# A two-block kernel (causal attention, then a routed mixture of experts): the last block is opened without GpSimd's drain at its end

## The chip, the cores and the metric

The kernel runs on one core of one Trainium2 chip. The metric is device time in microseconds of one execution, and the number before is the median of three runs. Five engines take part, each with an instruction queue of its own: TensorE (PE), VectorE (DVE), ScalarE (ACT), GpSimd (POOL) and SyncE (SP). Transfers run beside them on 16 DMA engines.

## What is computed

The reference, cut to what matters. The input is 4 sequences of 1024 tokens with 256 features; the result has the same shape.

```python
x = layernorm(x + attention(x))      # 16 heads of 16, causal, softmax
x = layernorm(x + ffn(x))

def ffn(x):                          # E = 16 experts, K = 2 per token, F = 128
    scores = sigmoid(x @ gate_w)
    _, selected = top_k(scores + expert_bias, K)
    w = scores[selected] / (scores[selected].sum() + 1e-20)
    shared = silu(x @ shared_gate_w) * (x @ shared_up_w) @ shared_down_w
    for e in range(E):
        g, u = split(x @ experts_gate_up[e])
        routed += comb[:, e] * (silu(g) * u @ experts_down[e])
    return shared + routed
```

## The kernel before

The program is written per engine, with semaphores by hand, in two blocks. A block (`nc.Block()`) holds one body for each engine. Its entry and its exit belong to a `with` context, and the exit of a block emits a barrier over all five engines. In the profile the instructions of that exit are booked to the line of the `with` statement in which the block was entered: L425 (`with ExitStack() as c1`) for the first block and L895 (`with ExitStack() as c3`) for the last one.

The barrier works through two semaphores, gather and release. Four engines (ScalarE, TensorE, DVE, SyncE) each run a DRAIN, which adds 1 to gather, and then a semaphore instruction that waits for release. GpSimd runs a DRAIN of its own, then a semaphore instruction that waits until gather is 4, then one that adds 4 to release. There are three such barriers: one at the start of the program (L1565), one at the end of the first block (L425) and one at the end of the last block (L895). Behind the last one the program has nothing more.

The first block projects q, k and v, and runs the attention in 16 steps (a batch and a group of four heads each). GpSimd masks probabilities there and copies values; it starts no transfer.

The last block does the output projection, the first layernorm, routing, the shared expert, the routed experts and the second layernorm, in this order:

- GpSimd sorts rows by expert with 64 indirect transfers (`scatter`, L1083: 40 for the first section of the tokens, 24 for the second) into `y_sorted`, and after each pair of expert blocks it sends the two results home with indirect transfers (`send_home`, L1091: 96 in all) into `z_back`.
- SyncE loads the sorted rows and later the two results of each tile (`load_z`, L1021).
- DVE adds the weighted results for each of the 32 tiles (`combine`, L1347 and L1350) and takes their statistics (L1353, L1355).
- GpSimd turns the statistics of four tiles into scale and shift (`second_deviation`, L1099 to L1104), in nine parts; the last two parts hold two tiles each.
- ScalarE applies them (`second_norm`, L1188) and sends the finished chunk to `out` (L1196) for seven of the eight chunks. SyncE sends the two halves of the last chunk (L1051).
- SyncE's last instructions of the block wait until all output transfers have landed (L1054):

```python
for c in range(CHUNKS):
    sp.wait_ge(out_stored[c], 16 * sum(part[0] == c for part in PARTS))
```

GpSimd's last instructions of the block are those of `second_deviation` for the last part. Everything that its indirect transfers write has been waited for earlier, since the results are read back from `z_back`.

Of the kernel before, what the change touches and what calls it, by code (L numbers as in the profile page):

```python
# [207 lines left out]
def build(nc, x, xT, Wq, bq, Wk, bk, Wv, bv, Wo, bo, gate_w, expert_bias, sg_w, su_w, sd_w, gu_w, down_w, out):  # L208
    with ExitStack() as ctx:
# [215 lines left out]
        with ExitStack() as c1:  # L425
# [226 lines left out]
            blk = c1.enter_context(nc.Block())  # L652
# [242 lines left out]
        with ExitStack() as c3:  # L895
# [110 lines left out]
            COUNT_BANK = 7  # L1006
            PARTS = [(c, 0, CT) for c in range(CHUNKS - 1)] + [(CHUNKS - 1, 0, CT // 2), (CHUNKS - 1, CT // 2, CT)]

            blk = c3.enter_context(nc.Block())

            @blk.sync
            def _(sp):
# [562 lines left out]
```

How the kernel before makes its waits and increments, by code:

```python
def wait_count(eng, sem, value):  # L163
    if isinstance(value, int) and value <= 0:
        return
    eng.wait_ge(sem, value)
# [2 lines left out]
def wait_apart(eng, sem, value, waited):  # L170
    eng.wait_ge(sem, value)
    eng.sem_inc(waited, 1)
# [165 lines left out]
        def turn_maxima(pe, i, qc, bank):  # L340
            pe.wait_ge(m_ready[qc], i + 1)
            dst = ps[0:3 * GH, bank, :].bitcast(BF16)
            for t in range(CT):
                mm = pe.transpose(dst[:, t * P:(t + 1) * P],
                                  m_parts[:, qc * CT + t].rearrange("p r h -> p (r h)"), ident_b[:, :])
            mm.then_inc(mT_ready[qc], 1)
# [1 line left out]
        def piece_maximum(dve, i, n, bank):  # L348
            qt, h, heads, half, w = MAXES[n]
            dst = m_neg[:, qt, h:h + heads] if half == 0 else m_neg_late[:, qt - CT, h:h + heads]
            if masked_by_vector(n):
                scores = ps[:, bank, 0:w]
                wait_apart(dve, score_max_ready, NM * i + n + 1, dve_waited)
                dve.tensor_tensor_reduce(out=scores, in0=scores, in1=wide_mask[:, CH - w:], scale=-1.0, scalar=-NEG,
                                         op0=ALU.add, op1=ALU.min, accum_out=dst).then_inc(reduced, 1)
                return
            dve.wait_ge(score_max_ready, NM * i + n + 1)
            dve.tensor_reduce(dst, ps[:, bank, 0:heads * w].rearrange("p (h k) -> p h k", h=heads), AX.X, ALU.max,
                              negate=True).then_inc(reduced, 1)
```

## Time and profile before

| | us |
|---|---|
| median of 3 runs | 894.93 |
| lowest and highest of them | 894.47, 896.44 |
| the profiled execution's own time | 893.04 |
| its span, first to last instruction | 891.3 |
| TensorE busy | 818.8 |
| DVE busy | 643.1 |
| ScalarE busy | 484.3 |
| GpSimd busy | 341.4 |

The page and its views count an engine as busy only with operations that it executes on data. Drains, branches and semaphore instructions run on an engine's sequencer (marked with a q, as POOLq); they appear where a single line is asked for, and in the chain and the waits, but not in the timeline or the busy times. The execution's own time is 1.7 us longer than its span; what lies outside the span isn't in the trace.

### The profile page before, as it was taken

The numbers are of one execution on the slowest core, as the hardware profiler recorded it, in microseconds if no ns is written. First come the engines' busy times: TensorE is split into PE (matmuls) and PEld (weight loads), VectorE is DVE, ScalarE is ACT, GpSimd is POOL, SyncE is SP. The second block draws the span as 40 slices with busy tenths as digits, with TensorE's granted clock in tenths as the row PEclk, the third lists the DMA queues.
The fourth block names the chain that finished last, engine by engine and source line by source line (L and its number), as shares of the span: only waits on it lengthen the run. The fifth ranks groups of instructions, "written<-read, shape, count | busy, mean of one in ns | idle before, by whom it ended". The sixth has DMA issues, their size and how long they took to land. (4 is left out here: it accounts for less than half of the span.)

```text
span 891.3 us, 17342 instructions
## 1 busy us (share of the span) xinstructions
PE 818.8 (92%) x5250; PEld 456.0 (51%) x5251; DVE 643.1 (72%) x1747; ACT 484.3 (54%) x728; POOL 341.4 (38%) x464
## 2 busy tenths in 40 slices
PE   7987999999999999999999999899996999999910
PEld 3554534434434343434443443389663888888810
DVE  6346899999999999999999996168775222227774
ACT  2443367667666766666666765656521344444443
POOL 5442412111221122111211122276477777655583
PEclk9999999999999999999999999999898899999965
DMA  8698363587556644685235500136133666567855
GB/s 275 211 251 190 124 91 41 105 144 105 90 109 108 97 63 107 120 145 71 37 39 72 74 1 4 50 124 204 43 108 106 211 185 187 174 183 233 273 181 207
DMA packets 90442, 114.60 MB, mean 129 GB/s; under 512 B 9232, under 2 KB 70928, under 8 KB 90384
## 3 DMA queue, kind: packets, MB, share of 16 engines
q1 hardware_dynamic: 74176, 85.22, 45.0%
q0 software_dynamic: 7680, 21.11, 6.5%
q10 hardware_dynamic: 8528, 7.50, 2.6%
q8 instruction: 36, 0.59, 0.3%
q14 instruction: 22, 0.18, 0.1%
HBM read 62.74 MB, written 50.66 MB: 127 GB/s over the span
## 5 line engine op out<-in xcount | busy, mean ns | idle before, releaser
L734 ACT ACTIVATE work<-ps 128x1024 f32<-128x1024 f32 (+3 forms) x384 | 293.8, 809 | 154.3 <-PE ps L805 151.9
L689 POOL TENSOR_SCALAR_AFFINE_SELECT work<-work 128x512 f32<-128x512 f32 x128 | 81.2, 634 | 371.7 <-ACT work L734 371.7
L358 DVE TENSOR_REDUCE m_neg<-ps 128x1 f32<-128x512 f32 (+2 forms) x304 | 195.1, 684 | 8.3 <-PE ps L334 5.3
L354 DVE CUSTOM_DVE_ANT_0 ps<-ps,wgu 128x384 f32<-128x384 f32 (+1 forms) x256 | 154.3, 649 | 15.2 <-PE ps L334 14.8
L334 PE MATMUL ps<-stacks 96*128 96x512 bf16 (+3 forms) x528 | 144.7, 329 | 8.0 <-DVE m_neg L354 4.6
L805 PE MATMUL ps<-stacks 99*128 99x512 bf16 (+3 forms) x528 | 125.4, 326 | 2.2 <-ACT work L734 1.7
L820 PE MATMUL ps<-work,vg 128*32 128x512 f32 (+3 forms) x1056 | 110.8, 497 | 0.4 <-POOL work L689 0.2
L1091 POOL DMA_INDIRECT z_back<-v_home,home x96 | 92.3, 962 | 47.5 <-ACT v_home L1165 27.4
L334 PEld LDWEIGHTS ps<-stacks 96*128 96x128 bf16 x528 | 49.2, 97 | 100.6 <-DVE m_neg L358 33.0
L1485 PE MATMUL ps<-wgu,work 128*128 x384 | 92.0, 383 | 0.0
L1333 DVE TENSOR_TENSOR work<-work,ps 128x256 f32<-128x256 f32 x48 | 20.2, 422 | 93.1 <-ACT work L1159 93.1
L1485 PEld LDWEIGHTS ps<-wgu,work 128*128 128x128 f32 x384 | 70.1, 192 | 8.0 <-issue 0.2
L805 PEld LDWEIGHTS ps<-stacks 99*128 99x128 bf16 x528 | 44.0, 98 | 53.9 <-ACT work L734 14.7
L1083 POOL DMA_INDIRECT y_sorted<-v_home,row_of x64 | 61.9, 966 | 23.1 <-issue 18.0
L615 PE MATMUL ps<-work,wqk 128*128 128x512 f32 x128 | 60.6, 613 | 7.5 <-DMA wqk<-in_Wq 5.6
L334 PE MATMUL ps<-wgu 96*128 96x512 bf16 (+3 forms) x240 | 65.9, 328 | 0.0
L505 POOL TENSOR_TENSOR work<-work 128x512 bf16<-128x512 f32 x32 | 36.4, 1156 | 66.5 <-ACT work L538 66.5
L805 PE MATMUL ps<-wgu 99*128 99x512 bf16 (+3 forms) x240 | 57.3, 326 | 0.0
L533 ACT ACTIVATE work<-ps,bqk 128x512 bf16<-128x512 f32 x32 | 21.8, 685 | 53.7 <-DMA qk_parts<-work 36.3
L820 PE MATMUL ps<-work 128*32 128x512 f32 (+3 forms) x480 | 50.4, 497 | 0.0
L1501 PE MATMUL ps<-wdn,work 128*128 x192 | 49.6, 381 | 0.8 <-DVE work L1339 0.8
L574 DVE SCALAR_TENSOR_TENSOR work<-ps,bqk,work 128x512 f32<-128x512 f32 x32 | 23.9, 749 | 35.8 <-ACT work L533 35.7
(142 smaller groups left out, 1156.0 us busy)
## 6 DMA issues: line engine op xcount, KB each, us to landing
stacks<-qk_parts SPq DMA_DIRECT2D x132, 128.0 KB, 6.8
work<-y_sorted SPq DMA_DIRECT2D x48, 260.0 KB
qk_parts<-work SPq DMA_DIRECT2D x32, 384.0 KB, 5.1
y_sorted<-wgu SPq DMA_DIRECT2D x7, 1560.0 KB, 7.9
work<-z_back SPq DMA_DIRECT2D x32, 256.0 KB, 3.8
wgu<-qk_parts SPq DMA_DIRECT2D x60, 128.0 KB, 6.2
work<-in_xT SPq DMA_DIRECT2D x8, 512.0 KB, 4.3
work<-in_x SPq DMA_DIRECT2D x8, 512.0 KB, 4.0
```

The costliest lines, as they stand in the source:

```text
L334: mm = pe.matmul(dst, qs[r][0:KS, h0 + m, qt * P:(qt + 1) * P], ks[r][0:KS, h0 + m, half * CH:half * CH + w], start=True, stop=not diag)
L354: dve.tensor_tensor_reduce(out=scores, in0=scores, in1=wide_mask[:, CH - w:], scale=-1.0, scalar=-NEG, op0=ALU.add, op1=ALU.min, accum_out ...
L358: dve.tensor_reduce(dst, ps[:, bank, 0:heads * w].rearrange("p (h k) -> p h k", h=heads), AX.X, ALU.max, negate=True).then_inc(reduced, 1)
L615: mm = pe.matmul(ps[:, t, :], wqk[:, t // 2, h, (t % 2) * P:(t % 2 + 1) * P], xt[c % 3][:, h, :], start=(h == 0), stop=(h == DC - 1))
L689: pool.affine_select(out=blk_, in_=blk_, compare_op=ALU.is_ge, fill=0.0, base=0, pattern=[[0, GH], [1, P]], channel_multiplier=-1).then_in ...
L734: act.activation(probs[:, s + 2 * pair:s + 2 * pair + 2, off:CH], ps[:, SCORE_BANK + 2 * pair:SCORE_BANK + 2 * pair + 2, off:CH], ACT.Exp, ...
L805: mm = pe.matmul(ps[:, SCORE_BANK + h, off:CH], ks[r][0:KM, h, kt * P:(kt + 1) * P], qs[r][0:KM, h, qc * CH + off:(qc + 1) * CH], start=Tr ...
L820: mm = pe.matmul(ps[32 * h:32 * h + 32, OUT_BANK, off:CH], vg[r][:, kt, h, :], probs[:, s + h, off:CH], start=(kt == 0), stop=(kt == CT * ...
L1083: pool.indirect_dma_start(out=y_sorted[g], out_offset=bass.IndirectOffsetOnAxis(ap=row_of[:, j, t:t + 1], axis=0), in_=y_rows_all[:, t, :] ...
L1091: pool.indirect_dma_start(out=z_back, out_offset=bass.IndirectOffsetOnAxis(ap=home[:, 2 * n + k:2 * n + k + 1], axis=0), in_=zs[n % ZS][:, ...
L1485: mm = pe.matmul(ps[:, 2 + r, 2 * F * k:2 * F * (k + 1)], ysT[r][:, h, k, :], wgu[:, bass.ds(e, 1), h, :].squeeze(1), start=(h == 0), stop ...
L1501: mm = pe.matmul(ps[:, 6 + r, D * k:D * (k + 1)], hxT[r][:, k, :], wdn[:, bass.ds(e, 1), :].squeeze(1), start=True, stop=True)
```

## The change

The last block is opened with `no_gpsimd_drain=True`.

```diff
             COUNT_BANK = 7
             PARTS = [(c, 0, CT) for c in range(CHUNKS - 1)] + [(CHUNKS - 1, 0, CT // 2), (CHUNKS - 1, CT // 2, CT)]
 
-            blk = c3.enter_context(nc.Block())
+            blk = c3.enter_context(nc.Block(no_gpsimd_drain=True))
 
             @blk.sync
             def _(sp):
```

In the built program this changes only the barrier at the end of that block; all other instructions and their order are the same. This is what each engine has there:

```
engine                  before                                after
ACT, PE, DVE, SP        DRAIN, which adds 1 to gather         DRAIN
                                                              EVENT_SEMAPHORE, which adds 1 to gather
                        EVENT_SEMAPHORE, waits for release    EVENT_SEMAPHORE, waits for release
POOL                    DRAIN                                 (none)
                        EVENT_SEMAPHORE, waits gather >= 4    EVENT_SEMAPHORE, waits gather >= 4
                        EVENT_SEMAPHORE, adds 4 to release    EVENT_SEMAPHORE, adds 4 to release
```

The first block and the barrier at the start of the program stay as they are.

## Rows read from the trace of the kernel before

**Rows 1.** The page: its head and the busy times by engine.

```profile
span 891.3 us, 17342 instructions
PE 818.8 (92%) x5250; PEld 456.0 (51%) x5251; DVE 643.1 (72%) x1747; ACT 484.3 (54%) x728; POOL 341.4 (38%) x464
```

**Rows 2.** Timeline from 880.5 us: start, duration, engine, line, operation.

```profile
880.51 3.16 SPq L1051 DMA_DIRECT2D out<-stacks  x2
...
881.95 0.19 POOL L1104 TENSOR_TENSOR second_moments<-second_moments,second_rstd 128x2 f32<-128x2 f32 x1
882.17 1.09 ACT L1188 ACTIVATE stacks<-stacks,second_moments,second_rstd 128x256 f32<-128x256 f32 x2 [1.69 <-POOL second_moments L1104]
```

**Rows 3.** Busy time of each engine by stretch, with clock, DMA share, GB/s.

```profile
880.00:884.00 4.00, 0.00 (x0) 0.00 (x0) 0.41 (x2) 1.58 (x3) 1.36 (x4) 0.50 0.53 178
884.00:886.00 2.00, 0.00 (x0) 0.00 (x0) 0.00 (x0) 0.00 (x0) 0.00 (x0) 0.50 0.40 135
886.00:888.00 2.00, 0.00 (x0) 0.00 (x0) 0.00 (x0) 0.00 (x0) 0.00 (x0) 0.50 0.00 0
888.00:892.00 4.00, 0.00 (x0) 0.00 (x0) 0.00 (x0) 0.00 (x0) 0.00 (x0) 0.50 0.00 0
```

**Rows 4.** Line L895: count, ns min/median/max, first and last start in us.

```profile
L895 POOLq EVENT_SEMAPHORE  x2: 17/17/17, 891.1 to 891.2; - x2
L895 PEldq DRAIN  x1: 1027/1027/1027, 850.6 to 850.6; - x1
L895 DVEq DRAIN  x1: 220/220/220, 880.3 to 880.3; - x1
L895 POOLq DRAIN  x1: 9152/9152/9152, 881.9 to 881.9; - x1
L895 ACTq DRAIN  x1: 1121/1121/1121, 882.2 to 882.2; - x1
L895 SPq COMPARE_BRANCH  x1: 41/41/41, 885.8 to 885.8; - x1
L895 SPq DRAIN  x1: 7/7/7, 885.9 to 885.9; - x1
L895 SPq EVENT_SEMAPHORE  x1: 17/17/17, 891.2 to 891.2; - x1
```

**Rows 5.** The chain that ended last, its last pieces: start, us, what.

```profile
881.91 0.24 POOLq L895
...
882.77 0.49 ACTq L895
```

**Rows 6.** Waits of SyncE: us in total, times, longest.

```profile
SPq L895 <- PEq L895: 5.3, 1, 5.3
...
SPq L1054 <- DMA out<-stacks: 1.5, 1, 1.5
```

**Rows 7.** Line L425, the end of the first block, columns as in rows 4.

```profile
L425 POOLq EVENT_SEMAPHORE  x2: 17/17/17, 575.8 to 575.8; - x2
...
L425 POOLq DRAIN  x1: 3264/3264/3264, 572.4 to 572.4; - x1
...
L425 DVEq DRAIN  x1: 464/464/464, 575.2 to 575.2; - x1
```

**Rows 8.** Timeline of GpSimd from 574 to 577 us.

```profile
573.54 2.09 POOL L407 TENSOR_TENSOR work<-work,bo_all 128x256 f32<-128x256 f32 x3
575.97 0.34 POOL L1071 IOTA v_home<- 128x128 int32 x1 [0.34 <-POOLq L425]
```

**Rows 9.** Groups of GpSimd by line: its indirect transfers; busy, mean ns, idle before.

```profile
L1091 POOL DMA_INDIRECT z_back<-v_home,home x96 | 92.3, 962 | 47.5 <-ACT v_home L1165 27.4 <-issue 19.2 <-DVE home L1328 0.9
...
L1083 POOL DMA_INDIRECT y_sorted<-v_home,row_of x64 | 61.9, 966 | 23.1 <-issue 18.0 <-DVE row_of L1299 4.0 <-POOL v_home L1071 1.1
```

**Rows 10.** Timeline of GpSimd from 854 to 858 us.

```profile
856.27 0.96 POOL L1091 DMA_INDIRECT z_back<-v_home,home  x1 [0.30 <-issue]
857.31 0.35 POOL L1099 TENSOR_SCALAR second_rstd<-second_moments 128x4 f32<-128x4 f32 x1
```

**Rows 11.** Line L1565, the barrier at the start: GpSimd's drain.

```profile
L1565 POOLq DRAIN  x1: 173/173/173, 0.4 to 0.4; - x1
```

## The prediction, made before the changed kernel had run

> **What bounds the end now.** The change touches only the last microseconds, so I read the views from the end backwards and use the middle of the kernel only as a yardstick. First the page's head: the span, first to last instruction, is 891.3 us, with TensorE busy 92% of it [rows 1]. None of that work is touched; TensorE's last matrix work lies well ahead of the stretch in question.
>
> Next the timeline from 880.5 us on [rows 2]. GpSimd's last recorded operation (L1104) starts at 881.95 and takes 0.19, so it ends at 882.14. ScalarE's last (L1188) ends at 882.17 + 1.09 = 883.26. SyncE issues the last output transfer right behind it. The table by stretches says the same of the end [rows 3]: no engine has recorded work after 884, the transfers stop before 886, and from 886 on there is neither work nor traffic. Yet the span runs to 891.3. More than 5 us are idle on every row that counts as busy.
>
> What fills them shows only where the sequencers' own instructions are listed, at L895, the `with` line to which the exit of the last block is booked [rows 4]. DVE's drain starts at 880.3 and takes 0.22; ScalarE's starts at 882.2 and takes 1.12 (until its ACTIVATEs are done); SyncE's starts at 885.9 and takes 0.007. GpSimd's starts at 881.9 and takes 9.152, so it ends at about 881.91 + 9.15 = 891.06; the chain of waits puts GpSimd's sequencer at L895 from 881.91, which gives the second decimal [rows 5]. All semaphore instructions of the barrier stand behind it, at 891.1 and 891.2. TensorE's started at 850.6 and was over after 1.03.
>
> SyncE's waits confirm who is late [rows 6]. It waited 1.5 us at L1054 for the output to land, and then 5.3 us at L895 for the barrier. The releaser named there is TensorE's sequencer, whose drain had been over since 851.6, so the name is a guess of the view; the only drain still running after 885.9 is GpSimd's. The chain of waits also stops at ScalarE's last ACTIVATE and books nothing to the drain, so the page's list by line hides this cost.
>
> **Is that long drain only waiting for GpSimd's operations?** The first block ends in the same sort of barrier, at L425, and gives the comparison [rows 7]. There GpSimd's drain starts at 572.4 and takes 3.264, ending at 575.66; its last operation (the group of L407 at 573.54 for 2.09 us) ends at 575.63 [rows 8]. The drain ended 0.03 us after the work. In the last block it ends 891.06 - 882.14 = 8.92 us after it. What lies between the two is GpSimd's indirect transfers: 64 of L1083 and 96 of L1091 [rows 9], all in the last block. The last of the 96 was issued at 856.27 and was done on GpSimd in 0.96 us; arithmetic followed at once, at 857.31 [rows 10]. So whatever the 8.92 us are, they did not keep GpSimd from small operations during the 25 us before.
>
> **The change part by part.**
>
> 1. GpSimd's drain leaves the end of the last block. The barrier then closes when the latest of the other arrivals comes in. Those are TensorE (851.6), DVE (880.5), GpSimd itself (after its last operation is handed out, about 881.9), ScalarE (883.3) and SyncE, whose branch to the block's end stands at 885.8 and whose drain starts at 885.9 [rows 4]. SyncE is now last, because it alone waits for the output. That cover ends there: no other engine hides anything behind it.
>
> 2. From the last arrival to the end of the span. Before: 891.29 (the timeline's span is 891.3) - 891.06 = 0.23 us from the drain's end. In the first block, DVE's drain was last: 575.2 + 0.46 = 575.7, and the first operations start at 575.97 [rows 7, 8], 0.3 us later. I take 0.27, between the two.
>
> 3. Four other engines get one more instruction each: the drain now carries no semaphore, and a semaphore instruction follows. Only SyncE's lies on the path. Such instructions take 0.017 us there [rows 4], and two neighbouring ones of SyncE (the branch and the drain) start 0.1 apart; so 0.02 to 0.1, and I take 0.07. Nothing else is queued behind it on SyncE.
>
> 4. Nothing moves in the program ahead of the block's end, so no queue, buffer or clock changes. The other two barriers keep their drains: at the start 0.17 us and at L425 hidden behind DVE's last work [rows 7, 11].
>
> The sum: the span ends at 885.9 + 0.01 + 0.07 + 0.27 = 886.25 instead of 891.3, which is 5.05 us less. From SyncE's side: of its wait of 5.3, 0.27 + 0.07 stay, leaving 4.96. I take **5.0 us**. The profiled execution took 893.04 with a span of 891.3, so 1.7 us lie around it; the new profiled time is 888.0. That execution was 1.9 us under the median of the three runs, 894.93. The same 5.0 off the median gives **889.9 us**, or -0.56%. The bounds of the sum alone are 4.9 (the larger values of items 2 and 3) and 5.1.
>
> **What the drain does in 8.92 us, and a rule beside it.** The two drains show 0.03 us behind ordinary operations, and 8.92 us behind a block with 160 indirect transfers. Nothing before shows which of two things that is: work that runs whether or not somebody asks, or work that the drain itself starts. The sum above assumes that after the change nobody inside the measured time asks. If someone does, the price lies between nothing saved and the whole 8.92 moved behind the barrier.
>
> The Trainium skill (PSUM — Partial Sum Buffer, Engine vs sequencer instructions) says that a drain waits for the engine to go fully idle. By that rule read with the recorded operations alone, the drain would end at about 882.2, ahead of SyncE, and the change would save nothing. The trace disagrees by 8.9 us: either GpSimd isn't idle when its recorded operations end, or the drain does more.
>
> **The rivals.**
>
> A. Nothing gained: the 8.92 us are work under way in GpSimd from 882.14 on, drain or not, and something behind the barrier but inside the measured time waits until GpSimd is idle. The end stays at 891.06 plus what followed it: profiled 893.0, median 894.9. For it: this kernel's time holds 1.7 us outside the span, so something is done there. Against it: that something was short, and GpSimd took arithmetic at once behind its indirect transfers [rows 10], which doesn't look like an engine with a backlog. The same time results if GpSimd's semaphore instruction were held in the drain's place.
>
> B. Slower: the 8.92 us start only when somebody asks for GpSimd's idleness, and the next to ask sits behind the barrier, inside the measured time. Before, the asking began at 882.14 and 3.8 us of the work lay beside the output transfer and SyncE's wait (885.9 - 882.14). Moved behind the barrier, it starts at 886.25 and ends at 895.17, 4.1 us later than 891.06: profiled 897.2, median **899.0**, +0.46%. It decides if the asking is inside the measured time at all; its start would have to be before 882.14 for the move to cost nothing. For it: the difference of 0.03 and 8.92 fits something that a drain does for indirect transfers. Against it: it needs a second wait for idleness, and the 1.7 us around the span leave little room for one.
>
> The Trainium skill names a place for such a wait. Runtime: NRT & Kernel Launch (The ~15µs preamble/postamble breakdown) lists a barrier behind the kernel in which all engines are waited for, about 1.5 us, and VectorE: DVE Perf Modes (The DRAIN you can't avoid) counts drains of some 12 ns on all five engines outside the kernel. By the first page, A or B would hold; by the 12 ns of the second, nothing is left to pay. No row here shows what lies outside the span.
>
> C. That the change does nothing at all would need GpSimd's drain still at the block's end. The built program has none there, so only A covers this case.
>
> **How the numbers follow.** A measurement of this kernel tells about 0.2% from no change, here 1.8 us. The forecast (the wait for GpSimd is gone and isn't paid again inside the measured time) gets 0.80, because the room outside the span is small and the idle gap is seen whole in the trace. A gets 0.11. B gets 0.07, as it needs both a drain that starts the work and a second asker. The last 0.02 is a part of the wait coming back, still faster. So faster 0.82, same 0.11, slower 0.07.
>
> The three runs of before spread over 2.0 us, from 894.47 to 896.44, and the profiled one lay 1.9 us under their median. A median of few runs after may well sit 1 us off on either side, which makes 888.4 to 891.4 around 889.9. To leave out no more than 2 in 10, I stretch it toward A: 888.3 to 892.6.
>
> **What the changed profile would show.** At L895 no drain of GpSimd; SyncE's drain near 885.9 with the semaphore instructions 0.1 to 0.3 us behind it; SyncE's wait at L895 down from 5.3 to about 0.3; a span of about 886.2; stretches up to 884 as before. If the span is 886.2 but the time outside it grew from 1.7 to 6.8, A holds; if it grew to about 11, B does. If the span is not shorter, GpSimd's semaphore instruction waits in the drain's place. A shift elsewhere, before 880 us, would make the prediction wrong in a way that it has no term for.

## The result and the profile after

The changed kernel takes 889.32 us (median of six runs, 887.19 to 891.82), before 894.87 (six runs, 894.02 to 896.79). The ratio is 0.9931, with a 95% interval of 0.9912 to 0.9950: 4.5 to 7.9 us less. (The ratios here and below are those on record with their intervals, and not quotients of the medians; that quotient is 0.9938 here.) The forecast of 889.9 us lies 0.6 us off, and its 5.0 us lie inside the interval.

Line L895 of the changed kernel, to be held against [rows 4] (count, ns min/median/max, first and last start in us):

```profile
L895 PEldq EVENT_SEMAPHORE  x2: 51/51/51, 852.5 to 887.0; - x2
L895 DVEq EVENT_SEMAPHORE  x2: 21/21/21, 881.4 to 887.0; - x2
L895 ACTq EVENT_SEMAPHORE  x2: 17/17/17, 884.2 to 887.0; - x2
L895 SPq EVENT_SEMAPHORE  x2: 17/17/17, 886.8 to 887.0; - x2
L895 POOLq EVENT_SEMAPHORE  x2: 17/17/17, 886.8 to 886.9; - x2
...
L895 DVEq DRAIN  x1: 220/220/220, 881.1 to 881.1; - x1
L895 ACTq DRAIN  x1: 1119/1119/1119, 883.0 to 883.0; - x1
L895 SPq COMPARE_BRANCH  x1: 41/41/41, 886.6 to 886.6; - x1
L895 SPq DRAIN  x1: 7/7/7, 886.7 to 886.7; - x1
```

There is no drain of GpSimd. Each of the other four has its drain and now two semaphore instructions, the first of which is the arrival: 852.5, 881.4, 884.2, and for SyncE 886.8. GpSimd's own stand at 886.8 and 886.9, and everybody is released at 887.0. SyncE is the last to arrive, as forecast. Its waits in the changed kernel, against [rows 6]:

```profile
SPq L1054 <- DMA out<-stacks: 1.4, 1, 1.4
...
SPq L895 <- PEq L895: 0.2, 1, 0.2
```

The wait at the exit went from 5.3 to 0.2 us; the wait for the output's landing is as long as it was (1.5 and 1.4). This 5.1 us is the gain, read inside each of the two executions.

The two spans, 891.3 and 887.0, differ by 4.3 only:

```profile
span 887.0 us, 17345 instructions
PE 817.8 (92%) x5250; PEld 455.8 (51%) x5251; DVE 643.0 (72%) x1747; ACT 484.2 (55%) x728; POOL 341.7 (39%) x464
```

The work ahead of the end was 0.8 us later in this execution than in that of before: DVE's drain starts at 881.1, not 880.3. Whole executions of one kernel differ by more than that, so I measure the end from a mark inside the same execution, the start of DVE's drain at L895 to the end of the span. It is 11.0 us before (891.3 - 880.3) and 5.9 after (887.0 - 881.1). The execution's own time was 888.77, 1.8 us over its span, against 1.7 before, which is the same within the rounding of the spans. Nothing was pushed out of the span.

### The profile page after: what moved, and what is told of

Read it like the earlier page. It is cut to its first block and busy times, and to the rows that moved or that the text cites. A ratio compares the mean times of both kernels' runs of the same rounds, so it can differ in the third digit from the quotient of the medians.

```text
span 887.0 us, 17345 instructions
## 1 busy us (share of the span) xinstructions
PE 817.8 (92%) x5250; PEld 455.8 (51%) x5251; DVE 643.0 (72%) x1747; ACT 484.2 (55%) x728; POOL 341.7 (39%) x464
## 5 line engine op out<-in xcount | busy, mean ns | idle before, releaser
L354 DVE CUSTOM_DVE_ANT_0 ps<-ps,wgu 128x384 f32<-128x384 f32 (+1 forms) x256 | 154.3, 649 | 15.3 <-PE ps L334 14.8
```

The lines of the kernel that those rows point to most:

```text
L354: dve.tensor_tensor_reduce(out=scores, in0=scores, in1=wide_mask[:, CH - w:], scale=-1.0, scalar=-NEG, op0=ALU.add, op1=ALU.min, accum_out ...
```

## The experiments

### The changed kernel once more

No edit. It was timed again beside further runs of the kernel before.

> The changed kernel once more, for a tighter ratio. Theory 1 (SyncE's wait for GpSimd's drain is gone, 5.0 us, nothing comes back): ratio 0.9944, about 889.9 against 894.9, and 1.7 to 1.8 us outside the span. Rival (something else gained too, since the medians first measured differ by 5.55): a ratio clearly under 0.993.

Measured: 891.07 against 894.98, ratio 0.9937 (0.9914 to 0.9961), own time 1.7 us over its span. The profiled execution of this very kernel had a span of 891.3 us, as long as that of before:

```profile
L895 DVEq DRAIN  x1: 220/220/220, 885.3 to 885.3; - x1
```

By the mark the end is 891.3 - 885.3 = 6.0 us, as in the first profile of it (5.9). Who compares single spans would have read "no gain" here. The rival, a second gain beside the drain, isn't supported: the interval holds 0.9944, the quotient of the medians is 0.9956, and no profile shows another difference.

### GpSimd's drain written back by hand

```diff
                 for k in range(len(PARTS)):
                     second_deviation(k)
+                pool.drain()
```

on top of the change, so that the exit's barrier keeps its new form.

> The changed kernel with a drain of GpSimd as the last statement of its body in the last block. Theory 1 (the drain alone is the cost): the drain lasts about 9.1 us again and starts near 882, SyncE waits 5.3 us at the exit, the time is that of before, 894.9. Rival (the cost belongs to the exit's barrier in its old form, drains that carry the semaphore, not to GpSimd's drain): about 889.5, with a short drain in the body.

Measured: 895.32 against 894.98, ratio 1.0009 (0.9990 to 1.0028). The drain at its own line, and SyncE's wait:

```profile
L1124 POOLq DRAIN  x1: 9150/9150/9150, 883.0 to 883.0; - x1
```

```profile
SPq L895 <- PEq L895: 5.4, 1, 5.4
```

The whole gain is gone with this one instruction (DVE's drain starts at 881.3, the span ends at 892.4: 11.1 us). The new form of the barrier isn't what helped.

### The drain behind the barrier

```diff
                 staggered(pe, [(1, lambda n, k2, r: experts(n, "gate_up")), (3, lambda n, k2, r: experts(n, "down")),
                                (0, turn_rows), (1, gate_up), (2, turn_hidden), (3, down)], PAIRS)
+        nc.gpsimd.drain()
```

> The changed kernel with a drain of GpSimd behind the barrier, as the last instruction of the program. Theory 1 (a drain starts the 8.9 us of work when it is reached): the drain lasts about 8.9 us from the barrier on, the span ends near 895.2, the time is about 898.2, slower than before. Rival (the work runs anyhow from GpSimd's last operation on and the drain only waits for its end): the drain lasts about 4.9 us, the span ends near 891.1, the time is that of before, 894.9.

Measured: 899.29 against 894.98, ratio 1.0040 (1.0024 to 1.0057), slower than before. The drain and the barrier ahead of it:

```profile
L1544 POOLq DRAIN  x1: 8895/8895/8895, 888.6 to 888.6; - x1
```

```profile
L895 POOLq EVENT_SEMAPHORE  x2: 17/17/17, 888.4 to 888.5; - x2
...
L895 DVEq DRAIN  x1: 220/220/220, 882.7 to 882.7; - x1
```

GpSimd's last operation ended at 884.5 in this execution. 4.1 us later the drain still found its full 8.9 us to do. So it isn't work that runs down by itself, which was the premise of rival A of the prediction. Rival B had priced just this, an asker behind the barrier, at 899.0 us; with the asker put there on purpose the time is 899.3. Against the changed kernel timed beside it the medians differ by 8.2 us (899.29 - 891.07), against the first measurement of the changed kernel by 10.0 (899.29 - 889.32). By the mark the end is 897.5 - 882.7 = 14.8 us, 8.9 more than the 5.9 of the changed kernel, which is the drain's own duration.

### A ladder of drains

```diff
                 write_ids(0, 0, TILES)
+                pool.drain()
                 add_bias(pool, 1)
...
                     for i in range(SCATTERS[0] if g == 0 else SENT_BEFORE):
                         scatter(g, i)
+                        if g == 0 and i in (0, 1, SCATTERS[0] - 1):
+                            pool.drain()
...
+                pool.drain()
                 for k in range(len(PARTS)):
                     second_deviation(k)
```

on top of the kernel before, whose exit keeps its drain.

> The kernel before with further drains of GpSimd in the last block: one before its first indirect transfer, one behind the first, one behind the second, one behind the fortieth, one behind the last of all 160; then the exit's own. Theory 1a (a drain works off the transfers issued since the last drain, 8.92 us / 160 = 0.056 us each): about 0, 0.06, 0.06, 2.1, 6.7 and 0 us beyond GpSimd's own work. Theory 1b (a fixed cost when there was any indirect transfer since the last drain): 0, then 8.9 four times, and 0 at the exit. Theory 1c (a fixed cost for every drain once the program has used an indirect transfer): 0, then 8.9 five times. Theory 2 (a drain waits for transfers in flight to land): 0, about 2.5 behind the first, second and fortieth, 2.5 behind the last, 0 at the exit. The whole execution gets longer by what lies on the path.

The three drains among the scatters (L1120), the last drain ahead of the arithmetic (L1125) and the one at the exit:

```profile
L1120 POOLq DRAIN  x3: 2757/3011/15736, 636.2 to 679.0; - x3
```

```profile
L1125 POOLq DRAIN  x1: 12649/12649/12649, 858.1 to 858.1; - x1
```

```profile
L895 POOLq DRAIN  x1: 309/309/309, 890.1 to 890.1; - x1
```

A drain's duration also holds the operations that were handed out and not yet done when it started. So I take what it lasts beyond GpSimd's last operation ahead of it: the drain's start and duration from the view of its line, the operation's end from the timeline. For L1125 that operation and the next one are

```profile
860.94 0.96 POOL L1091 DMA_INDIRECT z_back<-v_home,home  x1 [0.30 <-issue]
870.91 0.24 POOL L1099 TENSOR_SCALAR second_rstd<-second_moments 128x4 f32<-128x4 f32 x1 [9.01 <-issue]
```

so it is 858.1 + 12.65 - 861.9 = 8.9 us. In that way the six drains come out at 0.07 (no transfer yet), 1.5, 1.6 (one each), 3.2 (38), 8.9 (120), and 0.08 at the exit (none since the last drain). Theory 1c falls at the exit, 1b at one and at 38 transfers, 2 at 38 and 120. Theory 1a has the right order and the wrong numbers.

For a single transfer theory 2 is right in kind. Its 2.5 us count from the start of the operation that issues the transfer, and 1 to 1.2 us of that are the operation itself:

```profile
636.45 1.22 POOL L1083 DMA_INDIRECT y_sorted<-v_home,row_of  x1 [3.96 <-DVE row_of L1303]
```

```profile
y_sorted<-v_home,row_of POOLq DMA_INDIRECT x1, 2.7
```

This transfer landed 2.7 us after 636.45, at 639.1, and the drain behind it ended at 636.2 + 3.01 = 639.2. By the nanoseconds in the trace the drain ended 0.08 us behind the landing, and so did the second one behind its own. So those 1.5 us are the wait for the landing.

The one execution took 898.16 us. By the mark its end is 896.4 - 885.2 = 11.2 us, as in the kernel before; what its five added drains cost ahead of the mark can't be told from a single execution.

### Shorter and longer stretches

```diff
                         scatter(g, i)
+                        if g == 0 and i in (4, 14, 39):
+                            pool.drain()
...
+                    if n in (7, 17, 47):
+                        pool.drain()
```

on top of the changed kernel, the second addition at the end of the loop over `send_home(n)`. The other kernel has `(39,)` and `(27, 47)` in the same places.

> The changed kernel with six drains of GpSimd in the last block, behind stretches of 5, 10, 25, 40, 20 and 60 indirect transfers. The ladder gave 1.54 and 1.56 us beyond GpSimd's own work behind one transfer, 3.16 behind 38, 8.88 behind 120, 8.92 behind 160. Theory 1a (an offset and a price for each transfer since the last drain; from one and 38 transfers 1.5 us and 0.044 us each): 1.7, 2.0, 2.6, 3.3, 2.4 and 4.1 us. Theory 1d (a price by transfer until a ceiling near 8.9 us is met below 120 transfers; from 120 transfers at the latest 0.062 us each above 1.5): 1.8, 2.1, 3.0, 3.9, 2.7 and 5.2 us at the least. Theory 1e (the price depends on the sort of transfer, the home ones cost more): the first three as in 1a, the later ones clearly more for the same number.

> The changed kernel with three drains of GpSimd in the last block, behind stretches of 40, 80 and 40 indirect transfers. Theory 1a: 3.3, 5.0 and 3.3 us beyond GpSimd's own work. Theory 1d: 3.9, 6.4 to 8.9 and 3.9 us. Theory 1e: 3.3 for the first 40, and clearly more for the last 40.

The drains of the kernel with short stretches, then those of the kernel with long ones, and in the latter GpSimd behind its last indirect transfer:

```profile
L1119 POOLq DRAIN  x3: 6345/10296/15127, 637.9 to 679.3; - x3
```

```profile
L1125 POOLq DRAIN  x3: 8992/12918/17302, 732.3 to 860.2; - x3
```

```profile
L1119 POOLq DRAIN  x1: 16022/16022/16022, 673.8 to 673.8; - x1
```

```profile
L1125 POOLq DRAIN  x2: 7346/7968/8589, 791.4 to 853.1; - x2
```

```profile
856.14 0.96 POOL L1091 DMA_INDIRECT z_back<-v_home,home  x1 [0.30 <-issue]
860.55 0.24 POOL L1099 TENSOR_SCALAR second_rstd<-second_moments 128x4 f32<-128x4 f32 x1 [3.45 <-issue]
```

The last drain had 40 transfers to work off: 853.1 + 7.35 - 857.1 = 3.3 us. Behind the first 40, which are scatters and not sent home, it was 3.3 too, so at 40 the sort of transfer doesn't matter (1e falls). For 80 it was 6.6, against 5.0 by theory 1a and 6.4 at least by 1d. The stretches of 5, 10, 25, 40, 20 and 60 gave 1.7, 2.0, 2.5, 3.7, 2.7 and 5.0. Neither theory holds throughout. Theory 1a is within 0.1 us up to 40, but for the 2.7 and the 3.7 (it has 2.4 and 3.3), and too low for 60 and 80 (4.1 and 5.0). Theory 1d is nearer for 60 and 80 (5.2 and 6.4 at the least), but too high for 25 (3.0), for 60 and for the two 3.3 behind 40 (3.9). Its shape, a rise that ends at a ceiling, is kept; the offset of 1.5 us is taken up below.

The one execution of each took 896.36 us (short stretches) and 888.0 (long ones). By the mark, the short ones end 7.2 us behind the start of DVE's drain (894.6 - 887.4), the long ones 6.0 (886.3 - 880.3). The likely reason is the last drain, 5.0 or 3.3 us ahead of the arithmetic of the second layernorm, of which the section on early drains tells; no run changed that drain alone.

### No drain of GpSimd in either block

```diff
-            blk = c1.enter_context(nc.Block())
+            blk = c1.enter_context(nc.Block(no_gpsimd_drain=True))
```

on top of the change.

> Neither block drains GpSimd at its end. Theory 1 (at L425 GpSimd's drain ends 0.08 us behind its own work and at the same time as DVE's, with no transfers to work off, so it costs nothing that others don't cover): the first block's end moves by at most 0.1 us, the time is that of the changed kernel, ratio to before 0.994. Rival (every drain of GpSimd at a block's end costs a part of a microsecond or more): 0.3 to 1 us less than the changed kernel.

Measured: 889.89 against 895.43, ratio 0.9940 (0.9919 to 0.9961), the changed kernel's. The end of the first block in this kernel:

```profile
L425 POOLq EVENT_SEMAPHORE  x2: 17/17/17, 576.0 to 576.1; - x2
...
L425 DVEq DRAIN  x1: 464/464/464, 575.5 to 575.5; - x1
```

From DVE's drain to GpSimd's first semaphore instruction it is 0.5 us (575.5 to 576.0); before it was 0.6 (575.2 to 575.8, [rows 7]). The drain there cost nothing that can be told: GpSimd had issued no transfers, and in the kernel before its drain ended at the same time as DVE's (575.7).

### Early drains

Three kernels keep the exit's drain and let an earlier one do its work.

```diff
                 for n in range(PAIRS):
                     send_home(n)
                     for i in range(SENT_BEFORE + 2 * n, min(SENT_BEFORE + 2 * n + 2, SCATTERS[1])):
                         scatter(1, i)
+                    if n in (47,):
+                        pool.drain()
```

The second has `(27, 47)`, the third `n == 27`.

> The kernel before with one further drain of GpSimd behind its last indirect transfer, ahead of the second layernorm's arithmetic. Theory 1 (the drain works off the transfers once): 8.9 us beyond GpSimd's work near 857 to 866, under 0.1 us at the exit, SyncE's wait at L895 0.2 us. But the arithmetic of the nine parts starts 9 us late and keeps about 2.3 us a part, 20.6 us in all, so its end moves from 882.1 to at least 887: the time is about that of before, 894 to 896. Rival (the drain is hidden there beside DVE's additions): GpSimd catches up, the time is that of the changed kernel, about 889.5.

Measured with one drain behind the last transfer: 896.15 against 895.43, ratio 1.0018 (1.0004 to 1.0032). As expected the exit's drain is short and the wait there 0.2 us, and the 5 us come back ahead of it. GpSimd stands still for 9 us and then never catches up, down to its last operation:

```profile
869.07 0.24 POOL L1099 TENSOR_SCALAR second_rstd<-second_moments 128x4 f32<-128x4 f32 x1 [9.03 <-issue]
...
888.19 0.20 POOL L1104 TENSOR_TENSOR second_moments<-second_moments,second_rstd 128x2 f32<-128x2 f32 x1
```

That operation ends 5.1 us behind the start of DVE's drain (883.2), against 1.9 in the kernel before (882.14 - 880.3). There GpSimd stood idle for 3.68, 0.71 and 1.18 us during this arithmetic, waiting for DVE's statistics; these 5.6 us are what it can make up of the 9, and the 3.4 us left are close to the 3.2 by which it ends later. By the mark the end is 894.4 - 883.2 = 11.2 us, about that of the kernel before (11.0). The early wait costs as much as the one that it replaces.

> The kernel before (its exit drains GpSimd) with two further drains of GpSimd: one behind the 28th pair's results and one behind the last pair's, so that the last one has 40 indirect transfers to work off. Theory 1d: 3.3 us beyond GpSimd's own work behind the last pair, under 0.1 us at the exit. GpSimd then starts the second layernorm's arithmetic 3.1 us late, and it stands idle for 3.68 us ahead of 874.27 in the kernel before, which covers that: the time is that of the changed kernel, ratio about 0.994. Rival (a drain in the loop of the experts holds up the rows sent home and with them the chain behind it): ratio 0.997 to 1.003.

Measured with two: 890.03 against 894.88, ratio 0.9950 (0.9932 to 0.9967), below the rival's 0.997: the changed kernel's gain with the exit's drain still in place. At the exit:

```profile
L895 DVEq DRAIN  x1: 222/222/222, 882.4 to 882.4; - x1
L895 POOLq DRAIN  x1: 309/309/309, 884.1 to 884.1; - x1
```

The drain behind the last pair cost 3.3 us, inside the 3.68 us for which GpSimd stood idle ahead of 874.27 in the kernel before. The first drain had 120 transfers behind it in this kernel, and took 9.1 us beyond GpSimd's work without holding anything up in the end.

> The kernel before (its exit drains GpSimd) with one further drain of GpSimd behind the 28th pair's results. 40 indirect transfers are then left for the exit's drain, all landed some 25 us before. Theory 1d with the price for 40 as measured right behind them (3.3 us beyond GpSimd's own work): the exit's drain ends near 882.1 + 3.3 = 885.4, ahead of SyncE's arrival at 885.9, and the time is that of the changed kernel, ratio about 0.994 to 0.995. Rival (landed transfers are cheaper, the offset of 1.5 us was the landing of the last one): the exit's drain only 1.8 us beyond, the same time. Rival 2 (a drain at the exit costs the ceiling of 8.9 us whatever came before): ratio 1.000.

Measured with one, 20 pairs before the end: 889.90 against 895.21, ratio 0.9945 (0.9930 to 0.9960). The exit's drain again has work, 40 transfers that landed long before, and its place among the others is what matters:

```profile
L895 DVEq DRAIN  x1: 222/222/222, 882.1 to 882.1; - x1
L895 POOLq DRAIN  x1: 3576/3576/3576, 883.7 to 883.7; - x1
L895 ACTq DRAIN  x1: 1121/1121/1121, 884.0 to 884.0; - x1
L895 SPq DRAIN  x1: 7/7/7, 887.7 to 887.7; - x1
```

It ends at 887.3, before SyncE's at 887.7, and so costs nothing. Beyond GpSimd's last operation (it ended at 883.94) it took 3.3 us, the same as right behind the transfers. The rival with landed transfers at 1.8 falls, as does rival 2.

### Four transfers left

```diff
+                    if n in (27, 45):
+                        pool.drain()
```

> As the one before, with a second early drain two pairs before the end, so that four indirect transfers are left for the exit's drain, landed some 25 us before. If the 1.5 us behind one transfer are the drain's own offset: 1.6 to 1.7 us beyond GpSimd's own work. If they are the landing of the last transfer: 0.1 to 0.3 us.

```profile
L895 POOLq DRAIN  x1: 627/627/627, 888.2 to 888.2; - x1
```

GpSimd's last operation ended at 888.39, so the drain took 0.4 us beyond it. That is a little over what the landing theory said (0.1 to 0.3) and far from an offset of 1.5. The early drain in that kernel, with 36 transfers behind it, took 3.0. The one execution took 894.16 us; the mark gives 892.4 - 886.5 = 5.9 us for the end, so its drain at the exit is covered too.

All drains together, in us beyond GpSimd's own operations, from the kernels above. The last column tells of drains that stood right behind the last transfer, the one before it of drains whose transfers had landed some 25 us earlier:

```
indirect transfers        transfers          right behind
since the last drain      long landed        the last one
  0                       0.07 to 0.08 (there were none)
  1                       -                  1.5, 1.6
  4                       0.4                -
  5                       -                  1.7
 10                       -                  2.0
 20                       -                  2.7
 25                       -                  2.5
 36                       -                  3.0
 38                       -                  3.2
 40                       3.3                3.3, 3.3, 3.3, 3.7
 60                       -                  5.0
 80                       -                  6.6
120                       -                  8.9, 9.1, 9.1, 9.1
160                       8.9, 8.9, 8.9      8.9
```

One of the three 8.9 in the last row is the drain behind the barrier, counted from its own start.

With landed transfers the price rises by 0.08 us each: (3.3 - 0.4) / 36. Back to no transfer that gives 0.1, which is what was measured there. The drains right behind 36, 60 and 80 transfers lie on the same line (3.0, 5.0, 6.6), and by it the ceiling of 8.9 to 9.1 is met near 108 to 110.

Right behind fewer transfers the drain takes longer than that, and the landings in the trace show the larger part of the reason. The drain doesn't end before the last transfer has landed, which in the kernels above was 1.44 to 1.55 us after GpSimd's last operation. Behind 1, 5, 10, 25 and 38 transfers it ended 0.08, 0.25, 0.45, 1.06 and 1.68 us after that landing, so 0.04 us more for each; what these 0.04 are isn't shown. Two values lie over this, 2.7 behind 20 and 3.7 behind one stretch of 40. There the trace books no landing, but the last packets of GpSimd's DMA queue ended 1.5 and 1.7 us after its last operation, against 1.1 for the other stretches up to 40, so the likely reason is a later landing. All 160 transfers are of one size, so a price per transfer can't be told from a price per row.

## Why the prediction was right

**The reading of the end** held. The 9.15 us drain was the last of the arrivals to end, SyncE came second to last, and without the drain SyncE closes the barrier. One slip in it changes nothing: the chain books not nothing but 0.24 us to GpSimd's sequencer at L895 [rows 5]; the other 8.9 us are missing from it all the same. Writing the drain back by hand took back all of the gain.

**From the last arrival to the end**, the sum had 0.27 us, and 0.07 for the added semaphore instruction. Measured from SyncE's drain (886.7) to the end of the span it is 0.3. The new instruction follows the drain by 0.1 at the views' resolution, within the bounds. The wait of SyncE that is left was put at about 0.3 us and is 0.2. The forecast span of 886.2 us came out as 887.0 because this execution was 0.8 us later ahead of the mark.

**The sum of 5.0 us** compares with 5.1 by SyncE's wait and by the mark (11.0 - 5.9), and with 5.6, 3.9 and 5.5 between the medians of the three measurements without drains at the end (5.55, 3.91, and 5.54 in the kernel with neither block's drain). Their intervals all hold 5.0. That the first medians differ by half a microsecond more than the sum isn't a step that failed; no profile shows a second place. That the median came within 0.6 us of the forecast is partly luck: the repeat gave 891.07, and single executions of the changed kernel took 887.19 to 893.66.

**Nothing is paid behind the barrier**: the time outside the span stayed at 1.7 to 1.8 us. Rival A's premise is refuted by the drain behind the barrier, which still had its whole 8.9 us to do when it started 4.1 us after GpSimd's last operation. The argument given against A, that GpSimd took arithmetic at once behind its transfers, was weak: it did so in every kernel that had no drain there, and the 8.9 us were due all the same. Rival B's mechanism is real, the drain does the work when it is reached, but in the changed kernel nobody asks inside the measured time. That was the open condition, and the prediction argued it only from the small room of 1.7 us; the result is what settled it. What is done with those transfers after the measured time isn't visible here and stays open.

**What the 8.92 us are** was left open by the prediction. They aren't a fixed price: they grow by 0.08 us for each indirect transfer since GpSimd's last drain, up to about 9 us. What the hardware does in that time, and why there is a ceiling, no run here shows; where the text says that a drain works transfers off, only its duration has been seen.

## What to carry to other kernels

Where a program ends, or a block does, ask for the line of the exit and look at each engine's drain there: this one took 9.15 us and was in no busy time, no timeline, and the chain that ended last held 0.24 us of it. In these runs GpSimd's drain was dear only where GpSimd had issued indirect transfers since its last drain, and at the exit it costs only the time by which it ends behind the last other arrival. Where it must stay, an earlier drain at a point where GpSimd has slack takes its work over (ratio 0.9945, against 0.9931 to 0.9940 without the drain, with intervals that overlap), while one put ahead of work that others wait for moves the cost there (1.0018).

When the place of a change is one small stretch, measure from a mark inside each execution to the end of that stretch: two profiles of the same changed kernel had spans of 887.0 and 891.3 us, and ends of 5.9 and 6.0.

## What the runs showed of the hardware that wasn't expected

A drain of GpSimd takes time for each indirect transfer issued since its last drain even if they landed long ago: 40 of them took 3.3 us both right behind them and some 25 us later. Without a drain, small operations on GpSimd aren't held up: behind the last transfer they started within 0.1 us. A drain right behind a single transfer ended 0.08 us after the transfer had landed. Between 80 and 120 transfers the price stops rising (6.6, then 8.9 to 9.1), and 160 cost no more than 120.
